# A decoder layer's causal mask: a minimum on VectorE in place of mask products on TensorE

## The reference

```python
q = (x @ w_q).reshape(b, n, HEADS, DIM_HEAD).transpose(0, 2, 1, 3)
k = (x @ w_k).reshape(b, n, HEADS, DIM_HEAD).transpose(0, 2, 1, 3)
gates = jax.nn.sigmoid((x @ w_gate).reshape(b, n, HEADS, EXPERTS).transpose(0, 2, 1, 3))
sel = jnp.argmax(gates, axis=-1)
gm = jax.nn.one_hot(sel, EXPERTS, dtype=x.dtype) * gates
values = jnp.einsum('bhne,ehdk,bnd->bhnk', gm, value_experts, x)
sim = jnp.einsum('bhid,bhjd->bhij', q * SCALE, k)
causal_mask = jnp.triu(jnp.ones((n, n), dtype=bool), 1)
sim = jnp.where(causal_mask, jnp.finfo(sim.dtype).min, sim)
attn = jax.nn.softmax(sim, axis=-1)
out = jnp.einsum('bhij,bhjk->bhik', attn, values)
out = jnp.einsum('bhne,ehkd,bhnk->bhnd', gm, output_experts, out)
return out.sum(axis=1)
```

## Time and profile before

| | |
|---|---|
| time, median of 3 runs | 969.93 us (967.42 to 970.67) |
| the profiled execution's own time | 971.46 us |
| its span, from the first to the last instruction | 969.70 us |
| mean granted TensorE clock | 0.984 |
| TensorE busy | 911.0 us, 94% |
| VectorE busy | 616.9 us, 64% |
| GpSimd busy | 315.7 us, 33% |
| ScalarE busy | 308.0 us, 32% |

### The profile page before, as it was taken

How to read it: one execution, slowest core, us unless ns; L and a number is a source line. 1 busy time by engine, 2 the same in 40 slices (tenths; PEclk the granted TensorE clock), 3 DMA queues, 4 the chain that set the end, 5 groups by cost and what they waited for, 6 DMA issues and landing times.

```text
span 969.7 us, 15805 instructions
## 1 busy us (share of the span) xinstructions
PE 911.0 (94%) x6316; PEld 678.0 (70%) x6316; DVE 616.9 (64%) x932; ACT 308.0 (32%) x494; POOL 315.7 (33%) x309
## 2 busy tenths in 40 slices
PE   6989899999989989799999998999999989988998
PEld 3668678877744544699976786887775445448998
DVE  5758566567454564778868575765664454558887
ACT  4535555100245445101033355630003334440000
POOL 5112321211584677316610032300013553761000
PEclk9999999999999999889999999999999999989999
DMA  8112000444053453255530000021221010024653
GB/s 269 49 33 100 1 1 8 130 130 130 1 159 105 153 186 99 70 165 180 179 127 1 2 1 1 2 71 67 87 87 44 1 25 1 24 68 133 194 179 125
DMA packets 40959, 82.16 MB, mean 85 GB/s; under 512 B 12407, under 2 KB 17751, under 8 KB 40887
## 3 DMA queue, kind: packets, MB, share of 16 engines
q1 hardware_dynamic: 40887, 81.16, 26.6%
HBM read 61.65 MB, written 19.33 MB: 84 GB/s over the span
## 4 chain that ended last, share of the span: by engine, by line
PE 84%; DVE 8%; DMA 3%; issue 2%; ACT 1%; POOL 1%; SPq 1%; POOLq 0%; DVEq 0%
PE ps L1172 18%; PE ps L1539 11%; PE ps L1471 6%; DVE region L1027 5%; PE ps L1545 5%; PE ps L1391 5%; PE ps L1443 5%; PE ps L1345 5%; PE ps L1180 4%; PE ps L1412 4%; PE ps L1297 3%; PE ps L1359 3%; PE ps L1312 2%; PE ps L1485 2%; PE ps L1214 2%
## 5 line engine op out<-in xcount | busy, mean ns | idle before, releaser
L584 POOL TENSOR_TENSOR xT<-xT,region 128x1024 f32<-128x1024 f32 (+5 forms) x80 | 130.6, 1632 | 99.8 <-PE ps L1471 72.3
L1539 PE MATMUL ps<-expert_hi,k_hi 128*128 128x256 f32 x512 | 130.5, 291 | 9.4 <-DVE k_hi L1117 6.8
L1027 DVE TENSOR_REDUCE region<-ps 128x2 f32<-128x1024 f32 (+2 forms) x96 | 91.7, 956 | 60.0 <-PE ps L1418 36.6
L1539 PE MATMUL ps<-expert_lo,k_hi 128*128 128x256 f32 x512 | 128.8, 288 | 0.0
L1081 DVE COPY_PREDICATED region<-region,ps 128x512 f32<-128x512 uint32 x112 | 82.3, 735 | 72.0 <-PE ps L1172 71.5
L1539 PEld LDWEIGHTS ps<-expert_hi,k_hi 128*128 128x128 f32 x512 | 100.4, 196 | 13.4 <-DVE k_hi L1117 7.2
L1172 PE MATMUL ps<-expert_hi,wide_hi 128*128 128x512 f32 x256 | 103.9, 406 | 0.0
L1539 PEld LDWEIGHTS ps<-expert_lo,k_hi 128*128 128x128 f32 x512 | 101.3, 198 | 0.0
L1117 DVE TENSOR_TENSOR k_hi<-region 128x1024 fp32r<-128x1024 f32 x64 | 82.9, 1296 | 27.2 <-PE ps L1545 26.8
L1172 PE MATMUL ps<-expert_hi,wide_lo 128*128 128x512 f32 x256 | 100.0, 391 | 0.0
L1172 PE MATMUL ps<-expert_lo,wide_hi 128*128 128x512 f32 x256 | 99.9, 390 | 0.0
(11 more groups left out here) (157 smaller groups left out, 1721.1 us busy)
## 6 DMA issues: line engine op xcount, KB each, us to landing
region<-hot_rows SPq DMA_DIRECT2D x128, 128.0 KB, 3.7
expert_hi<-halves_kept SPq DMA_DIRECT2D x24, 512.0 KB, 3.8
expert_lo<-halves_kept SPq DMA_DIRECT2D x24, 512.0 KB, 5.1
halves_kept<-expert_hi SPq DMA_DIRECT2D x16, 512.0 KB, 5.3
halves_kept<-expert_lo SPq DMA_DIRECT2D x16, 512.0 KB, 6.1
expert<-in_value_experts SPq DMA_DIRECT2D x8, 512.0 KB, 4.5
expert<-in_output_experts SPq DMA_DIRECT2D x8, 512.0 KB, 4.4
gb<-scale_rows SPq DMA_DIRECT2D x16, 256.0 KB, 3.9
```

The lines of the kernel that those rows point to most:

```text
L584: pool.tensor_tensor(acc(c)[:, heads, lo:CH], acc(c)[:, heads, lo:CH], PT[:, k % RING, heads, lo:CH], ALU.add).then_inc(sem["added"], 1)
L1027: dve.tensor_reduce(mx[:, :, at:at + 1], ps[:, 6:8, 0:w], AX.X, ALU.max).then_inc(sem["s_max"], 1)
L1539: mm(ps[:, 4 + t // 2, t % 2 * D:(t % 2 + 1) * D], k_hi[n % 2][:, t * P:(t + 1) * P], w[:, slot, columns], start=(n == 0 and t % 2 == 0 an ...
```

## The change

The mask products of `transposed` go away. On a diagonal block VectorE now takes, after the exponential, the minimum of the first 128 columns of both heads with a triangle `seen` that holds 0 where the key lies after the query and 3e38 elsewhere: the new function `cut`, 128 partitions x 2 x 128 elements, in place. Weights of a diagonal block count as ready for TensorE's weigh and for both additions only after the cut (`weights_here`). `seen` is made once at the start: a DMA of its own into a buffer of its own, and one VectorE operation.

On VectorE cut u stands at the head of the turn of u + 1; the last pair's additions move from turn u to turn u + 1, behind the cut. The normalisation of the pair before moves to turn 11 in the pairs 2 and 3 and stays at turn 10 in the last pair.

```diff
-        side = sb("side", [P, 7, P], bf16)
-        ident_h, neg_q, neg_k, ones_b = side[:, 0:2], side[:, 2:4], side[:, 4:6], side[:, 6]
+        side = sb("side", [P, 5, P], bf16)
+        ident_h, neg_q, ones_b = side[:, 0:2], side[:, 2:4], side[:, 4]
+        seen = sb("seen", [P, P])
...
+        DIAGONAL = [u for u, (c, j) in enumerate(BLOCKS) if j >= TC * c]
...
+        def weights_here(eng, b, p, u):
+
+            if u in DIAGONAL:
+                until(eng, "cut", b, p * TT + DIAGONAL.index(u) + 1)
+            else:
+                until(eng, "pt_ready", b, p * NB + u + 1)
...
-                    sp.dma_start(side_f[to, 1:3, i, :], d["neg_f"][part]).then_inc(halves_in, 16)
+                    sp.dma_start(side_f[to, 1, i, :], d["neg_f"][part, 0]).then_inc(halves_in, 16)
+            sp.dma_start(seen[:, :], d["neg_f"][:, 1]).then_inc(halves_in, 16)
...
-                    until(pool, "pt_ready", b, p * NB + u + 1)
+                    weights_here(pool, b, p, u)
...
-            dve.tensor_copy(side[:, 0:6, :], side_f.rearrange("p w i s -> p (w i) s")).then_inc(casts, 1)
+            dve.tensor_copy(side[:, 0:4, :], side_f.rearrange("p w i s -> p (w i) s")).then_inc(casts, 1)
+            step(dve.tensor_scalar(seen[:, :], seen[:, :], 0.0, 3.0e38, ALU.is_ge, ALU.mult))
...
+                def cut(p, u):
+
+                    c, j = BLOCKS[u]
+                    lo = (j - TC * c) * P
+                    dst = PT[:, (p * len(RINGED) + RINGED.index(u)) % RING] if j else acc(c)
+                    until(dve, "pt_ready", b, p * NB + u + 1)
+                    dve.tensor_tensor(dst[:, :, lo:lo + P], dst[:, :, lo:lo + P],
+                                      seen[:, :].unsqueeze(1).broadcast_to([P, 2, P]), ALU.min
+                                      ).then_inc(sem["cut"], 1)
+
                 def add_up(u):
...
-                    until(dve, "pt_ready", b, p * NB + u + 1)
+                    weights_here(dve, b, p, u)
...
                     for u in range(NB):
+                        if u - 1 in DIAGONAL:
+                            cut(p, u - 1)
+                        elif p and u == 0:
+                            cut(p - 1, NB - 1)
+                        if p == PAIRS3 - 1 and u - 1 in RINGED:
+                            add_up(u - 1)
...
-                        elif u in RINGED:
-                            add_up(u)
                         if p and u == 5:
                             scaled(p - 1)
-                        if p and u == ROW_AT:
+                        if p and u == (ROW_AT + 1 if p + 1 < PAIRS3 else ROW_AT):
                             normalise(p - 1)
+                cut(PAIRS3 - 1, NB - 1)
+                add_up(NB - 1)
...
                         last = mm(ps[:, first + h, 0:w], ones_b[r, :], m_rows[r, i, query],
-                                  start=False, stop=not diagonal)
-                    if diagonal:
-                        for half in range(2):
-                            for h in range(2):
-                                r, hi = half_of(h), (half + 1) * HALF
-                                last = mm(ps[:, first + h, 0:hi], ident_h[r, half, :], neg_k[r, half, 0:hi],
-                                          start=False, stop=half == 1)
+                                  start=False, stop=True)
...
-                    until(pe, "pt_ready", b, g + 1)
+                    weights_here(pe, b, p, u)
```

More of the change, by code:

```diff
@@ L125, in decoder_layer @@
         bv2 = view(D)
-        side_f = view(6 * P).rearrange("p (w i s) -> p w i s", w=3, i=2)
+        side_f = view(4 * P).rearrange("p (w i s) -> p w i s", w=2, i=2)
         at[0] = (TT - 1) * H1 * NF
@@ L205, in decoder_layer @@
             s_ps=PAIRS3 * NB, s_max=PAIRS3 * NB, tile_max=PAIRS3, mxT_ps=PAIRS3, m_row=PAIRS3,
-            st_ps=PAIRS3 * NB, pt_ready=PAIRS3 * NB, av_used=PAIRS3 * NB, added=PAIRS3 * (NB - NC), added_b=NB - NC,
+            st_ps=PAIRS3 * NB, pt_ready=PAIRS3 * NB, cut=PAIRS3 * TT, av_used=PAIRS3 * NB, added=PAIRS3 * (NB - NC), added_b=NB - NC,
             den_ps=PAIRS3 * NC, den_sb=PAIRS3 * NC, o_sb=PAIRS3 * NC, dc_ready=PAIRS3,
@@ L234, in decoder_layer @@
         SETUP = 1
-        LOADS_KV, LOADS_SIDE, LOADS_HALVES, LOADS_FRONT, LOADS_LATER = 3, 1, 8, 3, 4
+        LOADS_KV, LOADS_SIDE, LOADS_HALVES, LOADS_FRONT, LOADS_LATER = 3, 1, 9, 3, 4
         N1_RUNS = [(0, 1, 0), (1, PAIRS1 - 1, 2 * V1W), (PAIRS1 - 1, PAIRS1, 4 * V1W)]
@@ L1430, in transposed @@
                     lo = max(0, j - TC * c) * P
-                    w, first, diagonal = CH - lo, 2 * (g % 2), j >= TC * c
+                    w, first = CH - lo, 2 * (g % 2)
                     if u == 0:
```

## The result

| | before | after |
|---|---|---|
| time, median | 969.6 us (967.42 to 970.67, 4 runs) | 993.16 us (989.4 to 993.45, 4 runs) |
| ratio | | 1.0238, 95% interval 1.0222 to 1.0253 |
| profiled execution, its span | 971.46, 969.7 us | 989.4, 987.6 us |

The changed kernel is slower by 2.4%. The forecast was 987 us; 993.16 lies inside the stated range of 974 to 995, just above the forecast's own 980 to 993 and inside the 990 to 994 of the half-clock rival. The sign and the place were right, the size 6 us short. Single executions of one kernel spread by some 3 us to either side of their median: in a later set those of before lay between 966.4 and 972.5, those of after between 988.8 and 995.0.

The account below looks back on a forecast made before the run. TensorE was taken to bound the kernel (94% busy, 84% of the chain), with VectorE pacing pair ends. Terms 16.4 + 2.3 + 1.1 - 2.9 = +16.9 on the profiled 971.46 gave 988.4, as a median 987 us; range 974 to 995.

Parts of the forecast that it names:

- half-clock rival: At pair ends, new TensorE waits halve its clock two to four times: +3.4 to +6.8 us, 990 to 994; chance 0.13.
- six pair ends, weigh 8 to 11: Ends of pairs 1 to 3, both samples: GpSimd's later additions hold VectorE's cuts, delaying TensorE's products by 16.4 us in all.
- fronts of the first pairs: First pair of each sample: cut 1 behind the last projection's low half makes weigh 1 late by 1.15, 2.3 us in all.
- fronts of the pairs 2 and 3: Later pairs' starts: sums of the pair before take up weigh 1's delay, so zero, at most 0.3 us each.
- last pairs' ends: End of each sample's last pair: GpSimd operations alternate with cuts 10 and 11, sums start 0.55 us later, 1.1 in all.
- mask products saved: TensorE at the 32 diagonal blocks 0 to 3: 0.09 us saved each, 2.9 us; blocks 8 to 11 counted as nothing.
- the hold: On VectorE, an operation with two SBUF inputs waits until GpSimd's running operation ends; taken in full for the cuts.
- no-hold rival: At pair ends GpSimd does not hold the cuts; late cut 9 and additions cost 6 there, +6 overall, 976 us; chance 0.10.
- Setup: At the kernel's start, the extra DMA and 128 x 128 conversion, under 0.5 us each ahead of waiting work, cost 0.

Follow-up runs that it names:

- e5: Changed kernel with GpSimd's additions of blocks 8 to 11 in pairs 1 to 3 cut to 8 columns per head, waits kept: 977.58 us, ratio 1.0073.
- e1: The changed kernel timed again with no edit, against the kernel before: 990.87 us, ratio 1.0234.
- e6: Changed kernel with extra TensorE products that nobody reads in front of the products that wait: 984.64 us, ratio 1.0149.
- e2: Kernel before without the mask products of the diagonal blocks and nothing in their place: 966.43 us, ratio 0.9965.
- e3: Changed kernel with cuts on blocks 0 to 3 only; blocks 8 to 11 keep their mask products: 967.38 us, ratio 0.9982.
- e4: Changed kernel with cuts on blocks 8 to 11 only; blocks 0 to 3 keep their mask products: 985.93 us, ratio 1.0175.
- e7: Changed kernel with cuts on blocks 0 to 3 only and cut 1 moved ahead of the projections' third low half: 965.76 us, ratio 0.9962.
- e9: Kernel before, all mask products kept and no cut, with only the change's order of additions and normalisation: 967.98 us, ratio 0.9990.
- e11: e7 with cuts on blocks 0, 1 and 2 only, so that block 3 keeps its mask products: 964.34 us, ratio 0.9963.
- e10: Kernel before with extra TensorE products filling waits behind the last pair and ahead of two output-expert steps: 966.01 us, ratio 0.9972.

## Why the prediction was right, and where its size was off

Each term against the lag within the two attentions of the profiled execution (21.4 in all, forecast 16.9):

| term | forecast | measured |
|---|---|---|
| six pair ends, weigh 8 to 11 | 1.6, 1.6, 3.9; 2.4, 3.0, 3.9: 16.4 | 1.29, 1.31, 3.27; 2.45, 2.61, 3.34: 14.3 |
| fronts of the first pairs | 2.3 | 2 x 1.06 = 2.1 |
| fronts of the pairs 2 and 3 | 0 | 4 x 0.16 = 0.6 |
| last pairs' ends | 1.1 | 2 x 1.08 = 2.2 |
| mask products saved | -2.9 | -0.9 (what is left of 21.4, not measured by itself) |
| late expert pieces | none | 0.99 + 0.90 = 1.9 |
| half clock behind pair 3 | rival | 1.25 |

The 4.5 between 16.9 and 21.4 are 1.9 of late pieces, 1.25 of clock, 1.1 at the last pairs' ends, 2.0 of saving that was not kept and 0.4 at the fronts, less 2.1 at the pair ends.

**The pair ends** were right in mechanism: GpSimd's later additions hold the merge and cut 10 at the places named, and e5 takes the hold away and with it 12 of 14 us, falls of the clock among them. Each walk came out 0.3 to 0.6 long, since the normalisations took 3.43 where I had 3.7 and the additions started a tenth earlier. The first sample's 2.4 for pair 1 is right for the wrong reason: I had split the difference between the piece and cut 9 going first; cut 9 did, the wait is 1.1 (e1, e6), and half clock made up the rest in this execution, which is luck.

**The no-hold rival** failed: with the hold gone the six pair ends cost 2 us, not 6, and the hold is worth 13 us of time, clock included (e5 against e1). I had charged the later addition a loss of its own that is nothing without its length.

**The half-clock rival** was real: four falls at pair ends, at its upper count. Its price was too high, 3.4 to 6.8; where TensorE waits for cut 11 anyway (pair 3) the fall costs nothing, and e6 puts the pair ends' and the following front's share at 3.2 (1.39 + 0.52 + 1.25). In e1's trace, where the falls lie elsewhere, they cost 1.5 in the middle of the first pair and 0.8 behind pair 3. By my own text this case was 990 to 994, which is where the time is.

**The saving** came out near the forecast without the cuts (e2: 3.0), but in part by luck, since the blocks 10 and 11 have a share that I had at nothing. With the cuts little of it is left. I let TensorE keep it in the blocks 0 to 3; but in the fronts weigh 1 now starts when cut 1 ends, so what the blocks 0 and 1 save only makes TensorE wait longer there.

**The step that was missing** is the one on GpSimd at the front. I followed cut 1 to weigh 1 and not to the addition that waits for it too, the expert piece behind that addition, its load, and ScalarE's queue: 1.9 us. e3 has this loss too; without cuts in the front (e4) or with cut 1 early (e7) it is gone.

**The last pairs' ends** cost twice the forecast, and more beside e9, where the new order alone gains 1.15 at each: the sums start 13.53 later than before (404.10 against 390.57), at a lag of 12.46 before that end.

Setup was 0 as said, as far as one trace tells (lag -0.10 at the first weigh, -0.83 to 1.10 in the other columns).

## What to carry to other kernels

Half of an engine's time being free says nothing of the places where it sets the pace; follow a new operation to everything that waits for it, on every engine, the slow helper's queue first, and count what each late start holds in turn. When an operation moves to another engine, try each of its places by itself: here three of the eight cuts of a pair could stay at a gain of 0.4% (e11), and the sum hid it.

## What the runs showed of the hardware that was not expected

GpSimd's select by index took 0.409 us over 128 x 256, where its addition of that shape took 0.73 in the kernel before (at 268.46). Filling TensorE's waits with products nobody reads gained 2.7 us (e10) and 6.2 (e6), though they add work; the 11 executions of e10 also lie within 2.9 us, the 23 of before beside them within 7.0. With the spread of single executions a difference of 3 us needs many of them: 11 or 12 against 23 gave intervals 0.2 to 0.3% wide.
